# Attention phase: the layer norms and loads of the next batch's x tiles moved to the ends of two head groups, and the five-pass loop over batches written out

## The reference, cut to what matters

```python
def _mha(Q, K, V, W_Q, b_Q, W_K, b_K, W_V, b_V, W_O, b_O):
    q = proj(Q, W_Q, b_Q)
    k = proj(K, W_K, b_K)
    v = proj(V, W_V, b_V)
    scores = jnp.einsum('bhqd,bhkd->bhqk', q, k) / jnp.sqrt(jnp.float32(D_K))
    attn = jax.nn.softmax(scores, axis=-1)
    out = jnp.einsum('bhqk,bhkd->bhqd', attn, v)
    ...
x = x + jnp.tanh(g_xattn[0]) * _L0_xattn_ref(_layernorm(x, axis=-1), ctx_1024, ctx_1024, ...)
x = x + jnp.tanh(g_ffn[0]) * _L0_ffn_ref(_layernorm(x, axis=-1), ...)
x = x + jnp.tanh(g_xattn[1]) * _L1_xattn_ref(_layernorm(x, axis=-1), ctx_1024)
x = x + jnp.tanh(g_ffn[1]) * _L1_ffn_ref(_layernorm(x, axis=-1), ...)
```

## Time and profile before

| what | value |
|---|---|
| median of three runs | 1733.74 us (1730.14 to 1733.93) |
| the profiled execution | 1735.12 us, its span 1733.3 us, 1.8 us outside the span |
| mean granted TensorE clock | 0.937 |
| attention, up to the last `attn_t` store | 866.6 us of the span |
| busy over the span | PE 1522.9 us (88%), DVE 1230.2, POOL 905.4, ACT 873.9 |

### The profile page before, as it was taken

How to read it: one execution, slowest core, us unless ns; L and a number is a source line. 1 busy time by engine, 2 the same in 40 slices (tenths; PEclk the granted TensorE clock), 3 DMA queues, 4 the chain that set the end, 5 groups by cost and what they waited for, 6 DMA issues and landing times. The chain is left out here.

```text
span 1733.3 us, 27279 instructions
## 1 busy us (share of the span) xinstructions
PE 1522.9 (88%) x7305; PEld 983.3 (57%) x7305; DVE 1230.2 (71%) x2149; ACT 873.9 (50%) x1433; POOL 905.4 (52%) x1162
## 2 busy tenths in 40 slices
PE   4789899998989999999726699999999938999997
PEld 3556565665656566565225355555555417888885
DVE  3566666776667677666476488888888826999985
ACT  3255455555555555545448455555555515555552
POOL 3166567656666765666600333434443215777774
PEclk9899999999999999998658899999999969999998
DMA  5826447382744638272090244444444344445420
GB/s 184 253 62 189 140 127 214 109 243 73 199 132 138 200 114 248 62 220 67 13 334 25 79 110 113 112 104 111 116 102 115 76 144 150 136 139 183 145 74 37
DMA packets 198401, 233.54 MB, mean 135 GB/s; under 512 B 97196, under 2 KB 114104, under 8 KB 194744
## 3 DMA queue, kind: packets, MB, share of 16 engines
q1 hardware_dynamic: 198328, 232.68, 46.3%
HBM read 135.86 MB, written 75.53 MB: 122 GB/s over the span
## 5 line engine op out<-in xcount | busy, mean ns | idle before, releaser
L501 ACT ACTIVATE a_probs<-a_sc 128x512 f32<-128x512 f32 x512 | 301.2, 596 | 312.3 <-PE a_sc L414 309.1
L556 DVE TENSOR_REDUCE a_negmax<-a_mx 128x1 f32<-128x512 f32 x512 | 336.7, 675 | 92.1 <-PE a_mx L397 90.4
L610 POOL TENSOR_TENSOR a_acc<-a_acc,a_probs 128x512 f32<-128x512 f32 x256 | 319.9, 1280 | 7.3 <-ACT a_probs L501 5.5
L610 POOL TENSOR_TENSOR a_acc<-a_probs 128x512 f32<-128x512 f32 x128 | 162.1, 1283 | 209.3 <-ACT a_probs L501 208.4
L397 PE MATMUL a_mx<-a_stack 96*128 96x512 f32 x512 | 229.0, 448 | 32.8 <-DVE a_negmax L556 19.9
L414 PE MATMUL a_sc<-a_stack 97*128 97x512 f32 x512 | 218.5, 429 | 18.1 <-DMA a_stack<-a_mrow 16.1
L993 PE MATMUL bank<-w_wgu,b_xq 128*128 128x512 bf16 x1024 | 228.1, 381 | 6.9 <-DMA b_xq<-b_xcode 6.7
L562 DVE RECIPROCAL a_attn<-a_den 128x128 f32<-128x128 f32 x128 | 120.8, 948 | 149.6 <-PE a_den L435 149.6
L993 PEld LDWEIGHTS bank<-w_wgu,b_xq 128*128 128x128 bf16 x1024 | 100.4, 98 | 129.7 <-DMA b_xq<-b_xcode 8.2
L397 PEld LDWEIGHTS a_mx<-a_stack 96*128 96x128 f32 x512 | 102.1, 199 | 104.9 <-DVE a_negmax L556 53.4
L1032 ACT ACTIVATE b_sig<-bank,b_tok 128x512 f32<-128x512 f32 x128 | 87.5, 683 | 91.6 <-PE bank L993 89.5
(11 more groups left out here) (177 smaller groups left out, 2657.1 us busy)
## 6 DMA issues: line engine op xcount, KB each, us to landing
a_stack<-spill SPq DMA_DIRECT2D x192, 256.0 KB, 4.9
spill<-a_part SPq DMA_DIRECT2D x64, 512.0 KB, 3.3
ctx_t<-a_ct SPq DMA_DIRECT2D x16, 1024.0 KB, 8.3
c_ct<-ctx_t SPq DMA_DIRECT2D x8, 2048.0 KB, 7.9
a_stage<-in_x_dram SPq DMA_DIRECT2D x32, 256.0 KB, 5.4
a_stage<-in_ctx_dram SPq DMA_DIRECT2D x32, 256.0 KB, 2.7
attn_t<-a_attn SPq DMA_DIRECT2D x32, 256.0 KB, 2.1
b_xin<-in_x_dram SPq DMA_DIRECT2D x32, 256.0 KB, 2.8
```

What stands on the lines that cost most here:

```text
L501: nc.scalar.activation(probs[:, k, j, :], sc[i % 2][:], ACT.Exp, scale=SCALE).then_inc(exp_done, 1)
L556: nc.vector.tensor_reduce(negmax[:, g % 2, j, t:t + 1], mx[i % 2][:], axis=AX.X, op=ALU.max, negate=True).then_inc(mx_done, 1)
L610: nc.gpsimd.tensor_tensor(acc[:, j], probs[:, 0, j] if k == 1 else acc[:, j], probs[:, k, j], ALU.add)\
```

## The change

The positions of the x tiles' load, statistics and norm steps become lists of four, one entry for each tile; the times of all other steps stay. POOL's lateness for the layer norm goes from 7 to 9. All five engines now write out every window (`unrolled`), with no loop and no register arithmetic.

```diff
+    def unrolled(self, engine, window, late={}):
+
+        order = self.order(late)
+        shifts = [shift for shift, _, _ in order]
+        for it in range(-max(shifts), self.batches - min(shifts)):
+            for shift, name, args in order:
+                if 0 <= it + shift < self.batches:
+                    window(it, shift, name, args)
...
-        at = dict(load=-760, load_step=16, ln1=-636, norm=-612, ln_step=24, tload=6, spill=20, act_norm=3, act_turn=4, dve_turn=8,
+        at = dict(load=(-860, -850, -740, -730), ln1=(-827, -822, -667, -662), norm=(-796, -786, -636, -626), tload=6, spill=20, act_norm=3, act_turn=4, dve_turn=8,
...
-                  recip=34, recip_step=16, norm_out=98, bias=108, store=118, pool_ln=7)
+                  recip=34, recip_step=16, norm_out=98, bias=108, store=118, pool_ln=9)
...
-            ck.add(at["load"] + i * at["load_step"], 9, "load", i)
-            ck.add(at["ln1"] + i * at["ln_step"], 8, "ln1", i)
-            ck.add(at["norm"] + i * at["ln_step"], 8, "norm", i)
+            ck.add(at["load"][i], 9, "load", i)
+            ck.add(at["ln1"][i], 8, "ln1", i)
+            ck.add(at["norm"][i], 8, "norm", i)
...
-                ck.run(sp, window)
+                ck.unrolled(sp, window)
```

More of the change, by code:

```diff
@@ L436, in window @@
                         last.then_inc(den_full, 1)
-                ck.run(pe, window)
+                ck.unrolled(pe, window)
             @block.scalar
@@ L507, in window @@
                                              bias=bias[:, 2, g:g + 1]).then_inc(biased, 1)
-                ck.run(act, window, dict(score=at["act_exp"], t=at["act_turn"], qk=at["act_qk"], v=at["act_v"], norm=at["act_norm"], mt=at["act_mt"]))
+                ck.unrolled(act, window, dict(score=at["act_exp"], t=at["act_turn"], qk=at["act_qk"], v=at["act_v"], norm=at["act_norm"], mt=at["act_mt"]))
             @block.vector
@@ L567, in window @@
                         nc.vector.tensor_tensor(attn[:, g % 2, :], pvb[:], attn[:, g % 2, :], ALU.mult).then_inc(attn_done, 1)
-                ck.run(dve, window, dict(max=at["dve_max"], t=at["dve_turn"], qk=at["dve_qk"]))
+                ck.unrolled(dve, window, dict(max=at["dve_max"], t=at["dve_turn"], qk=at["dve_qk"]))
             @block.gpsimd
@@ L611, in window @@
                             .then_inc(acc_done, 1)
-                ck.run(pool, window, dict(ln1=at["pool_ln"]))
+                ck.unrolled(pool, window, dict(ln1=at["pool_ln"]))
 def prepare_weights(nc, banks, keep0, keep1, N, w_o, b_o, w_gate, w_up, w_down, weight, bias_in, delta_w, delta_act,
```

## The result

The changed kernel takes 1709.68 us (median of 4 runs, 1707.63 to 1713.85) against 1733.01 us (1730.14 to 1733.93) of the kernel before in the same job: ratio 0.9863 [0.9844, 0.9882], 23.3 us less. The prediction said 1710. The profiled execution took 1708.97 us, its span is 1707.2 us.

The account below looks back on a forecast made before the run. PE bounds the kernel, lengthened in g0 by norm work and waits that batch 7 lacks. Gains 12.7 + 4.5 + 5.4 + 1.5 + 0.7, less 1.5, make 23.3 us: from 1733.74 to 1710 us, range 1704 to 1716.

Parts of the forecast that it names:

- Term 1: In g0, POOL's small norm steps leave the sums, so the seven `den` waits go: 12.7 us gained.
- Term 2: In g0, DVE's norm statistics leave the maxima for its idle time before the first reciprocal: 4.5 us gained.
- Term 3: Behind g3, two x loads leave the queue before the row of maxima: 5.4 us gained, plus 1.5 in the prologue.
- Term 4: At the five loop ends of the attention, writing out the windows gains 0.7 us, bounds 3 us either way.
- Term 5: New costs of moved norms, loads and statistics in g2, g3, g0 and the prologue: 1.5 us lost.
- g1, g2, g3: Sign of being right: these head-group stretches stay as long as before, to 0.3 us.
- The row stays late: Rival: behind g3 the row of maxima still lands late, the queue moving as many bytes; 1717 us, chance 0.17.
- The clock: Rival: without the `den` wait the granted clock stays up in g1, 12 us more gained; 1698 us, chance 0.07.
- A new wait in the gaps: Rival: late x tiles in g2 hold DVE's statistics, or loads slow the fill; 1720 us, chance 0.08.
- Code streaming: Rival: instruction fetches of five written-out windows stall PE or SP 8 us each; 1751 us, chance 0.04.

Follow-up runs that it names:

- e4: Changed kernel with POOL's small norm steps and ACT's norms back at their old positions in g0; 1723.51 us, ratio 0.9932 to the kernel before.
- e3: Kernel before, written out, with only the x loads at their new positions, statistics and norms at the old; 1722.02 us, ratio 0.9939.
- e6: Changed kernel with the layer norms of all four x tiles at the end of g3, none at the end of g2; 1708.24 us.
- e2: Kernel before with its old positions, but every window written out on all engines; 1738.22 us, ratio 1.0024.
- e9: Kernel before with its old positions, only SyncE's stream written out, all other engines in the loop; 1739.66 us, ratio 1.003.
- e1: Changed kernel's new positions, but the middle windows kept as a loop on all five engines; 1708.66 us, ratio 0.9847 to the kernel before.
- e10: e5 with the transposes of the first three x tiles moved into g0's last slots, the fourth to g1's slot 3; 1699.14 us.
- e12: e5 with two x-tile transposes moved into g0's last slots, the other two at g1's slots 0 and 3; 1689.28 us, ratio 0.974.
- e5: Changed kernel with all four x loads issued ahead of the batch's first spill, none at the end of g3; 1704.75 us, ratio 0.9828.
- e7: Changed kernel with VectorE's four reciprocals 22 positions apart, norm, bias and store moved accordingly; 1709.53 us, ratio 0.985 to the kernel before.
- e11: e5 with the x-tile transposes only drawn apart, to slots -2, 0, 2 and 4 of g1; 1701.17 us, ratio 0.9811.

## Why the prediction was right

**What bounds the kernel** was read rightly: batch 7's g0, without norms, was the measure of what could be had, and all six stretches came down to it within 0.6 us. The total, 23.3 us, is the sum predicted. The mechanisms of the three large terms show in the traces; their sizes differ from mine, and the hit to the last tenth is luck, as shown below.

Over the six g0 stretches the table under e4 gives 22.5 us: 7.8 up to the first score, 2.8 from there to `pv`, 12.0 from `pv` to `den`. The prediction had 5.4, 4.5 and 10.9 for them.

**Term 1 (12.7 us) stands.** The waits went, and e4 brings them and 12 us back. The printed waits were a little short: 12.0 us went between `pv` and `den` in six batches, where 10.9 us were printed as idle.

**Term 2 (4.5 us) was too large, but it is there.** I took 23.49 us, subtracted two sorts of printed waits and gave what was left to DVE, without a row that showed PE waiting that long. The one row, 0.28 us (in batch 2, not in batch 1 as I wrote), is the place, and its printed idle time is not its whole price. From the eighth score to the ninth around it, before:

```profile
286.91 0.40 PE L414 MATMUL a_sc<-a_stack 97*128 97x512 f32 x1
288.61 0.40 PE L414 MATMUL a_sc<-a_stack 97*128 97x512 f32 x1
```

And in the changed kernel:

```profile
275.46 0.40 PE L423 MATMUL a_sc<-a_stack 97*128 97x512 f32 x1
276.64 0.40 PE L423 MATMUL a_sc<-a_stack 97*128 97x512 f32 x1
```

The step takes 1.70 us and 1.18. It is 1.58 to 1.70 us in all six batches before, 1.51 to 1.69 in e3, and 1.16 to 1.19 in e4, e6 and the changed kernel: 2.7 us over the six, which come and go with DVE's statistics. The rest of my remainder of 4.8 us is 1.1 us of the wait before `den` and some 1 us that did not go: the first scores stand at 2.18 us on average, in batch 7 at 2.02. What the statistics would cost in the changed kernel, where POOL no longer holds `den`, no run tests; up to these 2.7 us is an estimate from the rows.

**Term 3 (5.4 us and 1.5 in the prologue, bounds 0 and 7.8) was too small.** The lateness of the first score fell from 3.47 us on average behind the g3 of batches 0 to 5 to 2.18 in the changed kernel, 1.29 x 6 = 7.8 us, the upper bound. With the 0.7 of term 4 and the 1.5 of term 5 off, e3 should have shown 6.1 us; it showed 10.6. Its trace gives 6.3 us of it to the first scores and 5.0 to g1. The mechanism was told only half rightly: the spill of the earlier trace rows takes 8.0 us in the changed kernel too, in place of the way half down to 6.2 that I had reckoned with. The one behind it, issued 6.6 us ahead of `den` in both, lands sooner. In the kernel before, issued at 368.84 us (KB, us to landing):

```profile
spill<-a_part SPq DMA_DIRECT2D x1, 512.0 KB, 5.9
```

In the changed one, issued at 354.29:

```profile
spill<-a_part SPq DMA_DIRECT2D x1, 512.0 KB, 4.5
```

What moved the row in this batch is SP's own list. DVE has the low part of k ready 12.2 us ahead of `den` before and 12.1 us after. But before, it was ready at 363.21 us and SP, still busy with the issues of x loads and a fill, issued the spill at 364.06; in the changed kernel it was ready at 348.75 and the spill issued at 348.91. The row is then issued 2.41 us ahead of `den` in place of 1.76. It also lands faster, in place of the 4.8 us of the earlier trace rows:

```profile
a_stack<-a_mrow SPq DMA_DIRECT2D x1, 8.0 KB, 4.3
```

The prologue's wait went from 8.30 to 7.06 us, but the first score of all came only 0.6 us earlier, at 73.55 in place of 74.15: ACT did norms of batch 1 at 50.60 and 51.79, ahead of the part of a projection that DVE then waited 1.17 us for, and PE stood 1.07 us for a maximum at 54.62 (part of term 5). The whole prologue up to its `den` is 1.3 us shorter.

**Term 4 (0.7 us) had the wrong sign with the old positions,** +4 us in e2 and 5 in e9, and is within the noise with the new ones (e1; 1.2 us by the traces). The bounds of 3 us on either side were too narrow. The Trainium skill (Runtime: NRT & Kernel Launch, section "Instruction fetch mechanics") has a taken branch stall for a fetch where its target is not in the pages at hand; by e1 the five loop ends cost nothing that the times can tell, and no instruction queue moved in the loop. That the old order loses by being written out is not a matter of TensorE's fetches either (e9).

**Term 5 (1.5 us) cannot be seen by itself.** DVE's idle time ahead of the first reciprocal is 2.08 us in the row shown, where I had said under 1, and e6, in which nothing is left of it, is no slower.

**g1, g2, g3** were to stay within 0.3 us. g1 came down by 3.7 us over its seven stretches (the clock stays low for 3.4 us in most batches where it was 6.8) and g2 by 1.5. I did not forecast that. PE's waits there did not shrink, and in e1 and e3 to e6, which leave g1 as it is, the seven stretches take 174.3 to 180.0 us (175.6 in the changed kernel, 179.3 before), by how long the clock stays low in each; what sets that stays open.

**The luck in the total.** In the profiled executions the attention shrank by 29.7 us: 22.5 in g0 and 1.3 in the prologue, which the prediction was about, and 5.9 in g1, g2, g3 and batch 7, which it was not. The part behind the attention took 3.5 of it back. That leaves 26.1 us; the profiled execution of the kernel before lay 2.1 us above the median beside the changed kernel, that of the changed kernel 0.7 under its own, and so the medians differ by 23.3. The places that I reckoned with came out 0.5 us from the sum; that the rest cancelled is chance.

**The rivals.** *The row stays late*: refuted, the first scores moved. *The clock*: refuted as stated. The `den` wait went, and the clock still falls in g1 in all seven batches, for a shorter time in most. The reason that I gave, the fall's place behind the transposes of g1, points to the waits at that place: in the changed kernel PE stood 1.28 and 1.65 us and then the clock fell. Stretches of 2 us there:

```profile
296.00:298.00 2.00, 0.37 (x2) 0.01 (x1) 2.00 (x4) 1.08 (x3) 1.81 (x2) 1.00 0.38 131
298.00:300.00 2.00, 1.98 (x5) 1.61 (x6) 1.48 (x3) 0.00 (x0) 0.68 (x1) 0.57 0.00 0
```

PE's row between the two:

```profile
298.02 1.38 PE L381 MATMUL a_work<-a_xt,a_w_q 128*128 128x512 f32 x3 [1.65 <-DVE a_xt L549]
```

In the first stretch DVE is busy for all 2.00 us and PE for 0.37, at clock 1.00; in the next the clock is 0.57. In e10 and e12 this wait is gone and so is the fall; the other idle time of g1 and the order of its work changed with it, so that the wait alone is not shown to be the cause. *A new wait in the gaps*: none appeared. *Code streaming*: not as stalls of 8 us; 13 packets of q8 and 16 of q14 moved from 300 to 650 us with at most half a microsecond at a first score (2.47 against 2.02).

So the time was right in the main because the total was bound by a measured stretch. Of its terms the wait for the row was 2.4 us too small, that for the maxima 1.7 too large, that for `den` 1.1 too small, and chance did the rest.

## What to carry to other kernels

A twin stretch in the same trace that lacks the suspected work measures the total; it does not say which of the pieces in it pays, and a remainder should not be given to a cause without a row that shows the wait. Better than a remainder is to measure from step to step: the printed idle time of 0.28 us stood for a step that was 0.5 us too long. A comparison made while another engine holds the end of the stretch cannot price a piece: in e3 and e4 what DVE gave up, POOL took. And where PE's clock falls at the same place in every batch, look at which engine it waits for just ahead: here, moving two transposes out of DVE's busiest moment was worth 15.5 us more (e12 against e5), waits and clock together, two thirds of the whole change.

## What the runs showed of the hardware

- In g1 of the changed kernel PE is idle for 3.3 us a stretch, the longest waits 1.28 and 1.65 us, and the granted clock falls once in each of the seven batches. In e12, with 1.4 to 1.6 us and no wait over 0.7, it never falls from 122.88 to 755.14 us. Neither figure decides alone: batch 4 of e7 (3.3 us, longest 1.65) and batch 1 of e11 (3.2 us, longest 1.35) have no fall, and e10 has a wait of 1.4 us in each g0 without one. Length, sum and place of the waits are not told apart by these runs.
- The fall in batch 1 of e7 cost 2.5 us of PE's time (22.91 us busy against 20.41 without a fall).
- The same DMAs in the same order, issued by a written-out SyncE, landed after 10.5 us in place of 8.0, the DMA share full in both (1.07 and 1.06) at 262 and 287 GB/s over the transfer. What decides between the two was not found.
- A spill's landing time stayed at 8.0 us although of the four x loads around it two were gone, one of them the load behind it; the spill after it gained 1.4 us.
